# Scores directly behind the probabilities, and maxima ahead of the other VectorE work, in the first cross attention of a two-layer decoder

## The chip, the cores and the metric

The kernel is one program on one core of a Trainium2 chip. Its time is the device time of one execution in microseconds (us), and a time given for a kernel is the median of several executions. A profiled execution is one more execution of the same program, taken by the hardware profiler. The engines are called as in the profile: PE is TensorE (PEld its weight loads), DVE is VectorE, ACT is ScalarE, POOL is GpSimd and SP is SyncE, which issues most DMAs. Each engine takes its instructions in the order in which they were written, and engines wait for one another on semaphores.

## What is computed

Sixteen sequences of 100 tokens of width 256 go through two decoder layers. Each layer is a mixer, a cross attention over 361 context rows and a mixture of experts, each added to its input. The change lies in the first layer's cross attention, which runs once for each of the 16 sequences:

```python
x = x + _L0_attn_ref(_layernorm(x, axis=-1), ...)          # gated recurrence and MLP
x = x + _L0_xattn_ref(_layernorm(x, axis=-1), ctx_1024, ctx_1024, ...)   # <- the change is in here
x = x + _L0_ffn_ref(_layernorm(x, axis=-1), ...)           # 32 experts, top 4, capacity, and a shared expert
x = x + _L1_attn_ref(...); x = x + _L1_xattn_ref(...); x = x + _L1_ffn_ref(...)

def _L0_xattn_ref(query, key, value, Wq, bq, Wk, bk, Wv, bv, Wo, bo):      # 16 heads of 16
    q, k, v = split(query @ Wq.T + bq), split(key @ Wk.T + bk), split(value @ Wv.T + bv)
    weights = softmax(einsum('bhqd,bhkd->bhqk', q, k) * inv_sqrt_d)
    out = einsum('bhqk,bhkd->bhqd', weights, v)
    return join(out) @ Wo.T + bo
```

## The kernel before

`stage_cross_experts` holds the first cross attention and, behind it, the first mixture of experts. The attention runs over 16 sequences `b`, and each sequence over 12 slots `k` (4 quarters of 4 heads, times 3 pieces of the 361 keys). In slot `k` PE makes one unit of scores in key-major form, ACT takes their exponential, and these are the probabilities of that slot (`prob_unit`, L2617; ACT L2866). The softmax needs the maximum of each row first. So one sequence ahead PE makes the scores of sequence `b + 1` in token-major form, in eight units `u` of two heads (`score_unit`, L2584), and VectorE takes their maxima (DVE L3031). After the last unit VectorE splits the maxima into two bfloat16 parts (`split_shift`, L3039 and L3041), PE turns them over (`shift_rows`, L2603), and ACT copies them in as extra rows of the queries (L2890), so that the next sequence's probabilities come out with the maximum taken off.

The eight score units go through four banks of `ps_score`, two banks to a unit: unit `u` waits until VectorE has the maximum of unit `u - 2` (semaphore `v_max`). Units 0 and 1 wait instead for ACT's copies of this sequence's values and shift rows out of the same banks (`a_val`, `a_shift`; ACT L2876 and L2890).

Beside this each slot has other work, set by the tables at the head of the stage. PE: `weigh_values` (L2630, slots 1, 4, 7 and 10), `logits` of sequence `b - 2` (L2671, slot 2, waits for ACT's copy L2885), for some sequences `positions`, `to_rows` of sequence `b - 1` (L2643, slot 4), `turn` (L2649, slot 6), `project` (L2657, slot 8), `values` of sequence `b + 1` (L2597, slots 9 to 11) and `turn_normal` of sequence `b - 1` (L2664, slot 11). VectorE: `to_rows` (L3047, L3049, slot 4), `project` of sequence `b - 1` (L3055 and statistics L3058, slot 8), `moments` (L3062, L3064, slot 9), `normalise` (L3073, slot 10), and in nine of the sequences parts of the routing, one part behind the other work of every second slot or so.

POOL has three things that hang on these. `set_base(b + 1)` (L3341) waits until VectorE has finished `project` of sequence `b - 1` (`v_out`). From sequence 8 on two indirect DMAs that scatter routing rows stand next in POOL's queue (`scatter`, L3366), and only then `root(b - 1)` (L3348), for which VectorE's `normalise` waits, and PE's `turn_normal` waits for that.

The tables and the order of the calls within a slot on PE, before:

```python
SCORE_AT = {0: 0, 2: 1, 3: 2, 4: 3, 5: 4, 6: 5, 7: 6, 8: 7}
AV_AT = {4: 0, 7: 1, 10: 2}
LAST_AV, SHIFT_B, SCALED, ROWS, TURN, OUT, SHIFT = 1, 0, 3, 4, 6, 8, 11
```

Below, "unit 3" is `score_unit(b + 1, 3)`, and the nine sequences 5 to 7, 9 to 11 and 13 to 15 are those with routing parts on VectorE.

## Time and profile before

| | us |
|---|---|
| median of 3 runs | 1654.94 |
| lowest, highest | 1651.81, 1658.08 |
| profiled execution, its own time | 1658.24 |
| its span, first to last instruction | 1656.1 |
| PE busy | 1481.8 (89%) |
| VectorE busy | 788.9 (48%) |
| ACT busy | 704.6 (43%) |
| POOL busy | 480.0 (29%) |

The span is what the instructions of the profiled execution took; 2.1 us lie around it. PE's clock was granted at 0.960 of full speed on the mean. The first cross attention is the stretch from 276.58 to 536.28 us, 259.7 us for the 16 sequences; sequence `b` is counted here from PE's first probabilities of that sequence to those of the next one.

### The profile page before, as it was taken

What the parts mean: (1) busy time and instruction counts of PE and PEld (TensorE: products, weight loads), DVE (VectorE), ACT (ScalarE), POOL (GpSimd) and SP (SyncE); (2) the same over time, 40 slices, a digit from 0 to 9 for tenths busy, and PEclk for the clock granted to TensorE, in tenths of its full rate; (3) what the DMA queues carried; (4) which work ended last, traced back from release to release, by engine and by line L of the source; (5) the groups of instructions that cost most, each with busy time, mean ns of one, the idle gap of its engine ahead of it and who ended that gap; (6) DMA issues with size and microseconds to landing.
All of it is one profiled execution on the core that took longest, in us unless ns stands there. A gap on an engine that the chain in (4) does not pass through costs nothing. (4 is left out here: it accounts for less than half of the span.)

```text
span 1656.1 us, 30297 instructions
## 1 busy us (share of the span) xinstructions
PE 1481.8 (89%) x11672; PEld 1113.7 (67%) x11672; DVE 788.9 (48%) x2238; ACT 704.6 (43%) x1473; POOL 480.0 (29%) x428
## 2 busy tenths in 40 slices
PE   6999997998887999999999957898799999949986
PEld 3666665666565668888888834565467667639885
DVE  6577575567665422222212236765566766541111
ACT  3463465666655212222222234455655565612222
POOL 2122122111434545666666520111101111012232
PEclk9999998999999999999999977999899999969999
DMA  7342567798671217777777626458477776439995
GB/s 300 124 147 94 161 159 127 139 158 139 111 127 34 78 47 192 195 197 192 192 199 201 151 52 160 80 107 166 93 144 128 121 129 121 74 102 345 312 301 159
DMA packets 252439, 250.86 MB, mean 151 GB/s; under 512 B 116724, under 2 KB 226700, under 8 KB 246796
## 3 DMA queue, kind: packets, MB, share of 16 engines
q1 hardware_dynamic: 210316, 221.13, 52.7%
q0 software_dynamic: 41984, 27.84, 9.8%
q8 instruction: 93, 1.52, 0.4%
q14 instruction: 46, 0.38, 0.1%
HBM read 194.10 MB, written 54.58 MB: 150 GB/s over the span
## 5 line engine op out<-in xcount | busy, mean ns | idle before, releaser
L2836 PE MATMUL cross_ps_score<-cross_q,cross_k 128*128 128x250 f32 x1024 | 221.8, 374 | 0.8 <-DVE cross_q L3317 0.8
L2836 PEld LDWEIGHTS cross_ps_score<-cross_q,cross_k 128*128 128x128 f32 x1024 | 194.3, 190 | 23.5 <-DVE cross_q L3317 1.0
L3326 DVE TENSOR_TENSOR cross_prob<-cross_act_,cross_ps_score 128x250 f32<-128x250 f32 x128 | 53.2, 416 | 266.7 <-ACT cross_act_ L3004 265.4
L1746 ACT ACTIVATE layer_parts<-layer_ps_prob 128x400 f32<-128x400 f32 (+1 forms) x192 | 97.0, 508 | 104.7 <-PE layer_ps_prob L1562 102.7
L3031 DVE TENSOR_REDUCE cross_nmax<-cross_ps_score 100x2 f32<-100x722 f32 x128 | 111.7, 902 | 61.0 <-PE cross_ps_score L2584 57.9
L3417 POOL DMA_INDIRECT x_sum<-cross_ye,cross_token x64 | 128.6, 2010 | 37.4 <-issue 19.0
L2866 ACT ACTIVATE cross_prob<-cross_ps_prob 128x400 f32<-128x400 f32 (+1 forms) x192 | 96.2, 508 | 93.4 <-PE cross_ps_prob L2617 91.8
L3004 ACT ACTIVATE cross_act_<-cross_ps_score 128x250 f32<-128x250 f32 x128 | 48.6, 380 | 179.0 <-PE cross_ps_score L2836 163.3
L2848 PE MATMUL cross_ps_prob<-cross_val,cross_prob 128*125 128x256 f32 x512 | 115.8, 379 | 0.0
L3407 POOL DMA_INDIRECT cross_xe<-ln_rows,cross_token x64 | 79.8, 1247 | 121.9 <-PE cross_ps_misc L2822 97.2
L3595 ACT ACTIVATE experts_h<-experts_ps_h,experts_b 128x128 f32<-128x128 f32 x160 | 45.7, 368 | 134.8 <-PE experts_ps_h L3564 122.7
L2848 PEld LDWEIGHTS cross_ps_prob<-cross_val,cross_prob 128*125 128x125 f32 x512 | 93.5, 188 | 12.8
L929 PE MATMUL mixer_bank<-mixer_ctx,packed_sb 128*128 128x361 f32 x256 | 86.7, 482 | 2.5 <-ACT xt L833 2.2
L1968 DVE CUSTOM_DVE_ANT_0 packed_sb<-layer_ps_score,layer_mask 100x361 bf16<-100x361 f32 x128 | 63.0, 532 | 38.3 <-PE layer_ps_score L1519 37.9
L3366 POOL DMA_INDIRECT row_token<-cross_choice,cross_row_put x64 | 64.5, 1008 | 31.6 <-issue 14.0
L1968 DVE CUSTOM_DVE_ANT_0 packed_sb<-layer_ring,layer_mask 100x361 bf16<-100x361 f32 x128 | 62.7, 528 | 22.0 <-PE layer_ring L1519 22.0
L3010 ACT ACTIVATE cross_ye<-cross_ps_prob,cross_weight 125x256 f32<-125x256 f32 x64 | 30.4, 474 | 94.4 <-PE cross_ps_prob L2848 92.6
L929 PEld LDWEIGHTS mixer_bank<-mixer_ctx,packed_sb 128*128 128x128 f32 x256 | 49.0, 196 | 30.4 <-issue 5.4
L814 ACT ACTIVATE mixer_full<-mixer_bank,packed_sb 128x361 f32<-128x361 f32 x64 | 34.8, 561 | 78.4 <-PE mixer_bank L929 78.4
L1557 PE MATMUL layer_ps_prob<-consts_sb,layer_mask 100*128 100x400 bf16 x192 | 64.1, 334 | 3.9 <-ACT layer_parts L1746 1.1
L1562 PEld LDWEIGHTS layer_ps_prob<-layer_m_q,layer_stacks 128*128 128x128 bf16 x720 | 51.9, 98 | 23.1
L3530 POOL DMA_INDIRECT out<-experts_ye,experts_put x20 | 31.7, 1587 | 111.2 <-DMA out<-experts_ye,experts_put 103.7
(471 smaller groups left out, 3097.1 us busy)
## 6 DMA issues: line engine op xcount, KB each, us to landing
packed_sb<-in_w SPq DMA_DIRECT2D x20, 1024.0 KB
experts_w<-in_w SPq DMA_DIRECT2D x20, 1024.0 KB
k_stack<-mixer_part SPq DMA_DIRECT2D x32, 541.5 KB, 4.0
cross_k<-in_wg SPq DMA_DIRECT2D x32, 512.0 KB
cross_k<-in_wu SPq DMA_DIRECT2D x32, 512.0 KB
cross_val<-in_wd SPq DMA_DIRECT2D x32, 512.0 KB
layer_stacks<-k_stack SPq DMA_DIRECT2D x30, 270.8 KB, 5.2
cross_k<-k_stack SPq DMA_DIRECT2D x25, 270.8 KB
```

The source lines that it names most:

```text
L929: ins = nc.tensor.matmul(bank[6 + m][:, 0:S2], prog.w(f"{LAYERS[l][1]}_wk", KD)[:, k, m * P:(m + 1) * P], ctx[s][:, k, :], start=(k == 0), ...
L1557: nc.tensor.matmul(ps_prob[k % 2][:, 0:GT], mask[b % M_BUFFERS][:, at:at + P], prog.c("tile_diag")[0:T, :], start=True, stop=False)
L1746: nc.scalar.activation(m_prob_sb[0:rows_, q4 % 2, t, :], ps_prob[k % 2][0:rows_, 0:GT], ACT.Exp, scale=DH ** -0.5).then_inc(m_prob, 1)
L1968: ins = nc.vector.tensor_tensor_reduce(m_scratch[:, h % HH, :], m_score[(u % 2) * 2 + j][0:T, 0:S2], mask[b % M_BUFFERS][:, 0:S2], -1.0, - ...
L2836: ins = nc.tensor.matmul(ps_pre[m][:, side, 0:CAP], w[s][:, k, m * P:(m + 1) * P], xt[s][:, k, :], start=(k == 0), stop=(k == KD - 1))
L2848: ins = nc.tensor.matmul(ps_sum[s][t][0:HALF], up[s][:, m, t * HALF:(t + 1) * HALF], wd[s][:, m, :], start=(m == 0), stop=(m == NUP - 1))
L2866: nc.scalar.activation(prob[0:rows_, q4 % 2, t, :], ps_prob[k % 2][0:rows_, 0:GT], ACT.Exp, scale=DH ** -0.5).then_inc(a_prob, 1)
L3031: nc.vector.tensor_reduce(nmax[b % 2][:, 2 * u:2 * u + 2], ps_score[0:T, (u % 2) * 2:(u % 2) * 2 + 2, 0:S2], AX.X, ALU.max, negate=True).t ...
L3326: nc.vector.tensor_tensor(up[s][:, m, :], act_[:, m % 2, :], ps_pre[m][:, 1, 0:CAP], ALU.mult).then_inc(v_gated[m][s], 1)
L3366: g.indirect_dma_start(prog.row_token, bass.IndirectOffsetOnAxis(row_put[:, c:c + 1], 0), choice[:, c, :], None).then_inc(scattered, 16)
L3407: g.indirect_dma_start(xe[s][:, t, :], None, prog.ln_rows, bass.IndirectOffsetOnAxis(token[:, 2 * e + t:2 * e + t + 1], 0)).then_inc(rows_ ...
L3417: g.indirect_dma_start(prog.x_sum, bass.IndirectOffsetOnAxis(token[:, 2 * e + t:2 * e + t + 1], 0), ye[s][:, t, :], None, compute_op=ALU.a ...
```

## The change

Two calls move within their slot. On PE, `score_unit(b + 1, ...)` is now called directly behind `prob_unit(b, k)`, ahead of the weighted values, logits, positions, rows, turn and project of that slot (and, in sequence 0, ahead of the turn and the projection of the spare queries). On VectorE, `score_unit(b + 1, ...)`, with `split_shift` behind the last unit, is now called ahead of `to_rows` and `project`. No instruction is added or removed, no table changes, and every wait stays with its instruction.

```diff
@@ PE
                         prob_unit(b, k)
                         if b == 0 and k == 0:
                             pe.wait_ge(consts_set, 1)
+                        if b + 1 < B and k in SCORE_AT:
+                            score_unit(b + 1, SCORE_AT[k])
                         if b == 0 and k in Q_TURN_AT:
                             query_turn(Q_TURN_AT.index(k))
...
                         if k == OUT and b > 0:
                             project(b - 1)
                         if b + 1 < B:
-                            if k in SCORE_AT:
-                                score_unit(b + 1, SCORE_AT[k])
                             if k == SHIFT:
@@ VectorE
+                        if b + 1 < B and k in SCORE_AT:
+                            score_unit(b + 1, SCORE_AT[k])
                         if k == ROWS and b > 0:
                             to_rows(b - 1)
                         if k == OUT and b > 0:
                             project(b - 1)
-                        if b + 1 < B and k in SCORE_AT:
-                            score_unit(b + 1, SCORE_AT[k])
```

PE, sequence 12, slots 2 to 4, before. L2617 are the probabilities, L2671 the logits, L2584 a unit of scores, L2630 the weighted values, L2643 the rows:

```order
L2617 MATMUL cross_ps_prob<-cross_q,cross_k 128x100 x4
L2671 MATMUL cross_ps_misc<-cent_t,xt 100x40 x2
L2584 MATMUL cross_ps_score<-cross_k,cross_q 128x361 x2
L2617 MATMUL cross_ps_prob<-cross_q,cross_k 128x100 x4
L2584 MATMUL cross_ps_score<-cross_k,cross_q 128x361 x2
L2617 MATMUL cross_ps_prob<-cross_q,cross_k 128x100 x4
L2630 MATMUL cross_ps_acc<-cross_prob,cross_val 32x100 x12
L2643 MATMUL cross_ps_misc<-packed_sb,cross_acc 100x128 x4
L2584 MATMUL cross_ps_score<-cross_k,cross_q 128x361 x2
```

The same stretch now:

```order
L2617 MATMUL cross_ps_prob<-cross_q,cross_k 128x100 x4
L2584 MATMUL cross_ps_score<-cross_k,cross_q 128x361 x2
L2671 MATMUL cross_ps_misc<-cent_t,xt 100x40 x2
L2617 MATMUL cross_ps_prob<-cross_q,cross_k 128x100 x4
L2584 MATMUL cross_ps_score<-cross_k,cross_q 128x361 x2
L2617 MATMUL cross_ps_prob<-cross_q,cross_k 128x100 x4
L2584 MATMUL cross_ps_score<-cross_k,cross_q 128x361 x2
L2630 MATMUL cross_ps_acc<-cross_prob,cross_val 32x100 x12
L2643 MATMUL cross_ps_misc<-packed_sb,cross_acc 100x128 x4
```

Unit 1 stands ahead of the logits, and unit 3 ahead of the weighted values and the rows; unit 2 has no other work in its slot and stays.

VectorE, sequence 12, slots 2 to 9, before. L3031 are maxima, L3047 and L3049 `to_rows`, L3055 and L3058 `project`, L3039 and L3041 the split, L3062 and L3064 `moments`:

```order
L3031 TENSOR_REDUCE cross_nmax<-cross_ps_score 100x2 x3
L3047 RECIPROCAL cross_rden<-cross_ps_misc 100x16
L3049 TENSOR_TENSOR cross_rows<-cross_ps_misc,cross_rden 100x256
L3031 TENSOR_REDUCE cross_nmax<-cross_ps_score 100x2 x4
L3055 TENSOR_TENSOR packed_sb<-cross_ps_misc,cross_base 100x256
L3058 BN_STATS cross_stats<-packed_sb 100x6
L3031 TENSOR_REDUCE cross_nmax<-cross_ps_score 100x2
L3039 CAST cross_split<-cross_nmax 100x16
L3041 TENSOR_TENSOR cross_split<-cross_nmax,cross_split 100x16
L3062 BN_AGGR cross_mv<-cross_stats 100x2
L3064 TENSOR_SCALAR cross_var<-cross_mv 100x1
```

The same stretch now:

```order
L3031 TENSOR_REDUCE cross_nmax<-cross_ps_score 100x2 x4
L3047 RECIPROCAL cross_rden<-cross_ps_misc 100x16
L3049 TENSOR_TENSOR cross_rows<-cross_ps_misc,cross_rden 100x256
L3031 TENSOR_REDUCE cross_nmax<-cross_ps_score 100x2 x4
L3039 CAST cross_split<-cross_nmax 100x16
L3041 TENSOR_TENSOR cross_split<-cross_nmax,cross_split 100x16
L3055 TENSOR_TENSOR packed_sb<-cross_ps_misc,cross_base 100x256
L3058 BN_STATS cross_stats<-packed_sb 100x6
L3062 BN_AGGR cross_mv<-cross_stats 100x2
L3064 TENSOR_SCALAR cross_var<-cross_mv 100x1
```

The maximum of unit 3 stands ahead of `to_rows`, and the maximum of unit 7 and both instructions of the split stand ahead of `project`.

## Rows read from the trace of the kernel before

**Rows 1.** Span and granted clock of the core.

```profile
core 0: 1656.1 us, clock 0.960
```

**Rows 2.** Stretches by sequence (3, 7, 9 to 12): length, then busy us (count) by engine.

```profile
326.35:341.15 14.80, 13.62 (x189) 9.98 (x189) 9.34 (x17) 9.58 (x24) 2.07 (x4) 1.00 1.08 213
...
386.86:403.35 16.49, 14.37 (x204) 10.72 (x203) 11.47 (x29) 9.68 (x24) 2.07 (x4) 1.00 0.70 125
...
419.28:435.64 16.36, 13.98 (x189) 9.96 (x189) 11.45 (x36) 9.62 (x24) 6.16 (x8) 1.00 0.77 125
435.64:452.41 16.77, 14.04 (x190) 10.03 (x191) 12.16 (x35) 10.55 (x26) 6.16 (x8) 1.00 0.80 120
452.41:470.47 18.06, 14.42 (x205) 10.60 (x204) 11.39 (x30) 9.30 (x23) 6.16 (x8) 1.00 0.66 113
470.47:486.38 15.91, 13.85 (x189) 9.92 (x190) 9.35 (x17) 9.62 (x24) 6.16 (x8) 1.00 0.76 128
```

**Rows 3.** Waits, 296 to 520 us: engine and line, releaser, us, times, longest.

```profile
DVE cross_nmax L3031 <- PE cross_ps_score L2584: 50.1, 31, 6.0
DVE cross_xf L3073 <- POOL cross_rstd L3348: 18.4, 14, 2.4
```

**Rows 4.** PE by time, sequence 12: start, us, instruction, count [idle before, releaser].

```profile
473.13 0.55 PE L2671 MATMUL cross_ps_misc<-cent_t,xt 128*100 128x40 f32 x4 [0.58 <-ACT xt L2885]
473.51 0.48 PE L2584 MATMUL cross_ps_score<-cross_k,cross_q 96*128 96x361 bf16 x2
...
476.74 0.37 PE L2649 MATMUL cross_ps_misc<-packed_sb,cross_rows 100*128 100x100 f32 x2
477.54 0.48 PE L2584 MATMUL cross_ps_score<-cross_k,cross_q 96*128 96x361 bf16 x2 [0.43 <-DVE cross_nmax L3031]
...
481.91 0.72 PE L2630 MATMUL cross_ps_acc<-cross_prob,cross_val 128*32 128x100 f32 x24
```

**Rows 5.** VectorE by time, sequence 12.

```profile
474.03 1.73 DVE L3031 TENSOR_REDUCE cross_nmax<-cross_ps_score 100x2 f32<-100x722 f32 x2 [1.65 <-PE cross_ps_score L2584]
...
480.48 0.42 DVE L3055 TENSOR_TENSOR packed_sb<-cross_ps_misc,cross_base 100x256 f32<-100x256 f32 x1 [0.25 <-PE cross_ps_misc L2657]
...
481.28 0.89 DVE L3031 TENSOR_REDUCE cross_nmax<-cross_ps_score 100x2 f32<-100x722 f32 x1
482.21 0.17 DVE L3039 CAST cross_split<-cross_nmax 100x16 bf16<-100x16 f32 x1
...
482.51 0.17 DVE L3062 BATCH_NORM_AGGREGATE cross_mv<-cross_stats 100x2 f32<-100x6 f32 x1
```

**Rows 6.** ACT by time, then POOL, sequence 12.

```profile
472.48 0.37 ACT L2876 COPY cross_val<-cross_ps_score 105x256 f32<-105x256 f32 x1
...
484.98 0.50 ACT L2866 ACTIVATE cross_prob<-cross_ps_prob 105x400 f32<-105x400 f32 x1 [2.19 <-PE cross_ps_prob L2617]
...
482.02 1.00 POOL L3366 DMA_INDIRECT row_token<-cross_choice,cross_row_put  x1 [0.31 <-POOL cross_base L3341]
483.33 0.99 POOL L3366 DMA_INDIRECT row_token<-cross_choice,cross_row_put  x1 [0.30 <-issue]
```

**Rows 7.** Sequence 10 by time: PE, VectorE, POOL and ACT.

```profile
447.72 0.72 PE L2630 MATMUL cross_ps_acc<-cross_prob,cross_val 128*32 128x100 f32 x24
...
452.18 0.39 PE L2664 MATMUL cross_ps_misc<-packed_sb,cross_xf 100*128 100x100 f32 x2 [1.29 <-DVE cross_xf L3073]
...
447.23 0.42 DVE L3055 TENSOR_TENSOR packed_sb<-cross_ps_misc,cross_base 100x256 f32<-100x256 f32 x1
...
448.77 1.00 POOL L3366 DMA_INDIRECT row_token<-cross_choice,cross_row_put  x1 [0.31 <-POOL cross_base L3341]
...
449.73 0.50 ACT L2866 ACTIVATE cross_prob<-cross_ps_prob 105x400 f32<-105x400 f32 x1 [1.13 <-issue]
```

**Rows 8.** PE by time: the spare queries' turn in sequence 0; unit 0 in sequence 4.

```profile
284.51 0.93 PE L2719 MATMUL cross_ps_misc<-packed_sb 100*128 100x100 f32 x4 [1.89 <-DVE packed_sb L3215]
...
342.81 0.48 PE L2584 MATMUL cross_ps_score<-cross_k,cross_q 96*128 96x361 bf16 x2 [1.30 <-DMA cross_k<-k_stack]
```

## The prediction

> **What bounds the kernel now.** I read the span first: 1656.1 us of the profiled execution, whose own time is 1658.24, 3.3 above the median of 1654.94 [rows 1]. My sum is made on the span, and its difference goes onto the median. Only the first cross attention is touched. Cut into its sequences, the attention shows two regimes [rows 2]. A sequence without routing ahead of number 8, such as 3, takes 14.80 us, of which PE is busy 13.62: PE sets the pace there, and what is left to win is 1.2 us. From sequence 8 on the same work takes 15.91 (number 12), with routing 16.36 to 18.06, while PE's busy time hardly moves (13.85 to 14.42). Something else ends last there.
>
> The waits name it [rows 3]. VectorE waits 50.1 us for scores, which looks like the prize, but it is idle time of an engine busy for 9.3 to 12.2 of some 16 us per sequence. The 18.4 us that `normalise` waits for POOL's root are another matter. In sequence 10 VectorE's `project` starts at 447.23, POOL's first scatter at 448.77, and PE's `turn_normal` runs at 452.18 after 1.29 idle [rows 7]: from `project` to `turn_normal` 4.95, and to the next sequence at 452.41 [rows 2] 5.18. In sequence 12 `project` starts at 480.48 [rows 5] and the next sequence at 486.38 [rows 2]: 5.90. I looked at all seven sequences, 8 to 14: two (10, 14) have 5.2, five have 5.8 to 5.9. So in these seven **the next sequence starts a fixed time after VectorE's `project`**, since base, two scatters, root, `normalise` and `turn_normal` hang on it in a row.
>
> Why two values: in sequence 12 ACT's exponential of the last slot starts at 484.98 after 2.19 idle, although PE made those probabilities at about 483.6; it comes 0.66 after the second scatter ended [rows 6]. In sequence 10 it comes at 449.73, in the middle of the first scatter, not late [rows 7]. The difference I find is when PE starts the third weighted values: 0.11 ahead of the first scatter in sequence 12 (481.91 and 482.02, [rows 4, 6]), 1.05 ahead in sequence 10 (447.72 and 448.77, [rows 7]). What PE signals in between seems to arrive late if those values run into the scatter. I can't say why, but can use it: **late kind** (5.9) and **clear kind** (5.2).
>
> **The change part by part.** Nothing is added, so only order counts. I replay one sequence, from PE's first probabilities at 0.
>
> *Unit 1 ahead of the logits.* PE idles 0.58 ahead of the logits of sequence 12, which start at 473.13, 2.66 after the start; unit 1 starts at 3.04 and VectorE's maximum at 3.56 [rows 4, 5]. Unit 1 itself needs the bank that ACT empties at 472.85, 2.38 after the start [rows 6]. So it starts at 2.43, its maximum at about 2.80: **VectorE is 0.75 ahead**. PE gains less: the unit occupies 0.32 (473.51 to the next row's start), the logits then start at 2.75 instead of 2.66, and the probabilities of slot 4 wait for the exponential of slot 2, which ACT, busy without a gap here, ends no earlier than 3.7. I keep 0.08 for PE.
>
> *Unit 5 ahead of the turn.* Before, PE idles 0.43 ahead of unit 5, waiting for the maximum of unit 3 [rows 4]. Now unit 3's maximum is taken ahead of `to_rows` and 0.75 earlier: that wait goes. But the turn needs `to_rows`, which is now behind the maximum: my replay has the rows ready at 6.4 and the turn at 6.5 instead of 6.27 (476.74), and the probabilities of slot 7 at 6.89 instead of 7.39.
>
> *Units 6 and 7 directly behind the probabilities.* Here the change takes cover away. Unit 6 waits for the maximum of unit 4, and the weighted values (0.66) and the project (0.9) no longer run meanwhile. One maximum takes 0.82 in a row of them (1.73 for two, overlapping). In sequence 3 or 12 this costs 0.15 at unit 6; with a routing part between the maxima, up to 0.35 at unit 7. Queued behind unit 7 on PE stand the project and all values of the next sequence. Net for PE: 0.35 earlier in a sequence without routing, 0.1 to 0.3 with it.
>
> *`project` behind the maximum of unit 7 and the split.* From the start of that maximum to the end of the split VectorE needs 1.23 (481.28 to 482.51, [rows 5]). `project` and its waiters, POOL's base, the scatters and the root, fall behind that. Against it stands the lead of 0.75, and where VectorE had waited for PE's project (0.25 in sequence 12) that gap too. Sum by kind:
> - sequences 8 and 12 (no routing): `project` at 9.95 instead of 10.01, so 0.06 less. The values now start 0.4 ahead of the scatter, still nearer to the late kind; next start 0.06 to 0.08 less.
> - 9 and 13: `project` 0.55 later (1.23 less the lead of about 0.7). The values are then 1.3 ahead of the scatter: the clear kind, 0.65 back. Each 0.10 less.
> - 10 and 14: 0.49 later, clear already, nothing to give back: each **0.48 more**.
> - 11: either unit 1's maximum leads here too (its `project` 0.2 later, clear: 0.5 less) or its signal is held by the scatters of slots 1 to 3 (0.5 more). I take 0.
> Together 8 to 14: -0.14 - 0.20 + 0.96 + 0 = **+0.6**.
>
> *Sequences 0 to 7.* Here the scatters don't exist, and `normalise` has about 0.9 of slack in sequence 3, so the later `project` is hidden by the values of slots 9 to 11; without that cover it would cost the same 0.5. Sequence 2 gains 0.35. So would 3, but 4 waits 1.30 for keys from DMA [rows 8], whose transfers start with sequence 3, so 3 gives its gain back; 4 gains 0.3. 5 and 6 gain 0.2 and 0.25. 7, whose unit 1 stood behind logits and positions, 0.4. 1 gains 0: two wide subtractions on VectorE stand between its maxima. In 0, unit 5 goes into the 1.89 that PE idles ahead of the spare queries' turn [rows 8], and a later wait for ACT's copy takes half of it back: 0.3. Sequence 15 makes no scores. Together **-1.8**.
>
> The waits that SP's queue holds (the stores of `normalise`'s rows, the next keys) move by these same tenths.
>
> *A rule weighed.* In sequence 12 the first scatter, with the split's cast inside it, took 1.00, and the second, with none, 0.99 [rows 5, 6]. The Trainium skill (SBUF — State Buffer, section "Who interferes with whom") says that casts on VectorE can take the port pair that it shares with GpSimd, and whoever starts first then blocks the other for the whole instruction. The change moves the split out of the scatters. By that rule up to a cast of 0.17 would come back in each of seven sequences, 1.2 us in all; by the rows 0.01 each. The sum goes by the rows.
>
> **Sum.** +0.6 - 1.8 = -1.2 on the span: 1654.9, and 1654.94 - 1.2 = 1653.7 for the median. Bounds of what the trace doesn't show: sequences 8 and 12 turning clear would give 0.7 each; 9 and 13 staying late would cost 0.65 each; 11 is 0.5 either way; PE's tenths in 0 to 7 lie between 0 and 0.7 a sequence. That is 1649.5 to 1657. The runs before spread by 3 to either side of their median.
>
> **The rivals.**
> *It works in full.* PE's waits for maxima vanish and nothing comes in their place: 0.35 in each of 14 sequences, 4.9, and the five late sequences turn clear, 3.5: 1646.5. For it: all scatters do move away from the values if `project` moves later. Against it: `project` moves later, and PE's start then doesn't count. From the point where `project` doesn't move and the scatter is still clear, it decides. Chance 0.12.
> *POOL's chain pays in full (slower).* Place: `project` behind unit 7's maximum and the split, sequences 8 to 14. If VectorE's lead doesn't come, because unit 1's signal reaches it no earlier than before (ACT's copies, or the scatters of slots 1 to 3), `project` is 1.23 later in each of seven: +8.6, with nothing won in 0 to 7, 1663.5; with half of the lead gone and the late kind cleared, some 1659. For it: VectorE is busy without a gap from unit 1's maximum to `project` in the routing sequences, so nothing there gives way. Against it: in sequence 12 VectorE did see unit 1's scores as soon as they were made (474.03), between scatters. It decides once less than about 0.5 of the 0.75 arrives. Chance 0.13.
> *The order doesn't matter.* The waits just change places and all ends within a few tenths, 1654.9. This lies inside my forecast's range.
> *Clock.* Granted clock falls to half at 284.5 in sequence 0, behind the 1.89 idle. A unit of scores in that gap may or may not shift this; it is worth up to 1 us either way. Chance that it decides: 0.03.
>
> **How the numbers follow.** Forecast 1653.7 with chance 0.72 (the unmoved case within it), the full gain 0.12, POOL's chain 0.13, the clock 0.03. A range of 1648 to 1659.5 holds the forecast with its bounds and the runs' spread, and leaves out most of the full gain and about two thirds of the slow case: some 0.2. A measurement of this kernel can tell about 0.5% from no change, 8.3 us. Below 1646.7 lies about half of the full gain, 0.06; above 1663.2 a little under half of the slow case, 0.05; the rest, 0.89, is no change that can be told.
>
> **What would show it.** Right: unit 1 on VectorE 2.8 after the start of a sequence; unit 5's wait for maxima gone and a wait of the turn for rows (L2649 behind L3049) in its place; units 6 and 7 waiting for maxima in routing sequences; `project` 0.5 later in 10 and 14 and these sequences 0.5 longer; 9 and 13 of the clear kind; sequences 2 to 7 shorter by 0.2 to 0.4. Wrong: sequences 8 to 14 shorter by more than PE's tenths (then the chain from `project` isn't what starts the next sequence), or sequence 3 longer (then the lost cover of units 6 and 7 weighs more than the removed wait), or a difference outside the first attention.

## The result and the profile after

| | median | lowest to highest | runs |
|---|---|---|---|
| before | 1653.91 us | 1646.31 to 1664.28 | 22 |
| the change | 1658.96 us | 1652.13 to 1664.62 | 22 |

The ratio is 1.0037, with a 95% interval of 1.0024 to 1.0051. The change is slower, by 5 to 6 us, where the prediction had it 1.2 us faster. The time lies in the forecast's range, just under its upper end; the sign was wrong.

First the span and the clock of the change (before: [rows 1]), then its stretches by sequence (before: [rows 2]), from sequence 0 to 14. The columns are start and end, length, busy us (count) of PE, PEld, VectorE, ACT and POOL, granted clock, DMA share, GB/s.

```profile
core 0: 1656.8 us, clock 0.950
```

```profile
278.83:297.40 18.57, 16.10 (x166) 10.23 (x165) 11.51 (x27) 11.25 (x22) 1.74 (x2) 0.91 0.90 150
...
326.94:341.50 14.56, 13.68 (x189) 9.69 (x189) 9.36 (x17) 9.53 (x24) 2.07 (x4) 1.00 1.08 212
...
386.38:404.73 18.35, 16.13 (x203) 11.28 (x204) 11.68 (x29) 9.68 (x24) 2.07 (x4) 0.91 0.62 115
...
420.56:436.74 16.18, 13.74 (x191) 9.63 (x190) 11.37 (x36) 9.79 (x24) 6.15 (x8) 1.00 0.75 125
436.74:453.88 17.14, 13.96 (x192) 9.65 (x191) 12.52 (x36) 9.90 (x25) 6.13 (x8) 1.00 0.81 119
453.88:473.69 19.81, 17.40 (x206) 12.28 (x204) 11.67 (x30) 9.90 (x24) 6.14 (x8) 0.83 0.60 102
473.69:489.00 15.31, 13.58 (x191) 9.60 (x190) 9.37 (x18) 9.79 (x24) 6.14 (x8) 1.00 0.81 133
```

Two stretches stand out. Sequence 7 takes 18.35 (16.49 before) and 11 takes 19.81 (18.06), and both have a granted clock under 1.00, which none of the sequences 1 to 14 had before. Sequence 3 is 0.24 shorter, 9 and 12 are 0.19 and 0.60 shorter, 10 and 14 are 0.37 and 0.51 longer. (By the same profiles 4 is 0.63 shorter, 0 is 1.43 shorter, and 14, at 0.99, has a fallen clock in its last tenths.)

What happened in sequence 7 around unit 6, by time, and then VectorE ahead of it (start, us, instruction, idle before and releaser):

```profile
395.91 0.91 DVE L3031 TENSOR_REDUCE cross_nmax<-cross_ps_score 100x2 f32<-100x722 f32 x1
396.05 0.13 PEld L2584 LDWEIGHTS cross_ps_score<-packed_sb,up 96*128 96x128 bf16 x2 [1.36 <-DVE cross_nmax L3031]
396.06 0.79 PE L2584 MATMUL cross_ps_score<-packed_sb,up 96*128 96x361 bf16 x2 [1.22 <-DVE cross_nmax L3031]
...
396.77 1.23 PE L2630 MATMUL cross_ps_acc<-cross_prob,cross_val 128*32 128x100 f32 x24
```

```profile
393.50 0.25 DVE L3047 RECIPROCAL cross_rden<-cross_ps_misc 100x16 f32<-100x16 f32 x1
393.78 0.42 DVE L3049 TENSOR_TENSOR cross_rows<-cross_ps_misc,cross_rden 100x256 f32<-100x256 f32 x1
394.12 0.36 DVE L3155 TENSOR_REDUCE cross_prior_add<-cross_any_hot 100x32 f32<-100x128 bf16 x1
394.40 0.68 DVE L3157 TENSOR_REDUCE cross_pos<-cross_prod 100x16 f32<-100x512 f32 x1
394.99 0.19 DVE L3159 TENSOR_TENSOR cross_prior<-cross_prior,cross_prior_add 100x32 bf16<-100x32 bf16 x1
395.09 1.72 DVE L3031 TENSOR_REDUCE cross_nmax<-cross_ps_score 100x2 f32<-100x722 f32 x2
```

Unit 6 now stands directly behind the probabilities and waits 1.22 for the maxima of unit 4. VectorE takes them at 395.09, behind the rows and part 11 of the routing (394.12 to 395.09). Behind the wait PE's matmuls are slow: the pair of scores takes 0.79 where it takes 0.48 elsewhere, the weighted values 1.23 where they took 0.72 [rows 4]. A mean clock of 0.91 over 18.35 us is some 3.4 us at the lower level, 1.2 GHz.

Sequence 11 has two such stretches. The second lies behind unit 6's wait, as in 7. The first begins with the sequence, behind another wait: `turn_normal`, the last work of sequence 10, waits 2.06 for `normalise`, where it waited 1.29 [rows 7].

```profile
453.65 0.40 PE L2664 MATMUL cross_ps_misc<-packed_sb,cross_xf 100*128 100x100 f32 x2 [2.06 <-DVE cross_xf L3073]
```

```profile
453.88:457.31 3.43, 3.43 (x42) 2.53 (x41) 0.91 (x2) 3.10 (x9) 2.08 (x4) 0.50 0.68 137
...
464.14:467.55 3.41, 3.31 (x34) 2.13 (x35) 2.28 (x8) 0.50 (x1) 0.00 (x0) 0.50 0.93 121
```

By this one pair of profiles the attention (sequences 0 to 14) takes 242.9 us before and 243.7 after, 0.7 more. The medians are 5 apart. So there were two questions: do sequences 7 and 11 decide, and where do the other 4 us come from?

### The profile page after: what moved, and what is told of

It reads as the page before. It is cut to its first block and busy times, and to the rows that moved or that the text cites. A ratio compares the mean times of both kernels' runs of the same rounds, so it can differ in the third digit from the quotient of the medians.

```text
span 1656.8 us, 30297 instructions
## 1 busy us (share of the span) xinstructions
PE 1492.4 (90%) x11672; PEld 1118.3 (67%) x11672; DVE 790.9 (48%) x2238; ACT 703.5 (42%) x1473; POOL 478.8 (29%) x428
## 5 line engine op out<-in xcount | busy, mean ns | idle before, releaser
L3031 DVE TENSOR_REDUCE cross_nmax<-cross_ps_score 100x2 f32<-100x722 f32 x128 | 111.8, 903 | 50.8 <-PE cross_ps_score L2584 50.5
```

What stands on the lines that cost most here:

```text
L3031: nc.vector.tensor_reduce(nmax[b % 2][:, 2 * u:2 * u + 2], ps_score[0:T, (u % 2) * 2:(u % 2) * 2 + 2, 0:S2], AX.X, ALU.max, negate=True).t ...
```

## The experiments

These theories were put up. **A**: sequences 7 and 11 (the wait for unit 4's maxima and the clock). **B**: POOL's chain in 8 to 14, fed later because `project` stands behind unit 7. **C** and **L**: outside the attention. **M**: ordinary executions of the attention are worse than the profiled one. All times of sequences are from one profile of each kernel. Steps (a) to (d) in the expectations are the four paragraphs of the prediction's change part by part: unit 1, unit 5, units 6 and 7, `project`. A condition in a diff stands on both engines unless it says otherwise, and the old place has the opposite condition.

### One engine, or one kind of sequence

`positions_old` keeps the old order in the sequences with `positions` (7, 11 and 15), `positions_new` has the new order in them alone:

```diff
-if b + 1 < B and k in SCORE_AT:
+if b + 1 < B and k in SCORE_AT and counted_group(b) is None:      # positions_old
+if b + 1 < B and k in SCORE_AT and counted_group(b) is not None:  # positions_new
     score_unit(b + 1, SCORE_AT[k])
```

`tensor_half` has the diff's two hunks in PE's loop, `vector_half` its two hunks in VectorE's.

> The change as it is, but with before's order on TensorE and VectorE in the three sequences of the first attention that also make the positions (7, 11 and 15). Theory A (the whole loss sits in sequences 7 and 11: TensorE waits 1.2 us for the maxima of unit 4 behind the rows and a part of the routing on VectorE, and its granted clock falls to half): no slower than before, 1651 to 1654 us (before 1653.9, the change 1659.0), lengths of sequences 7 and 11 back at 16.5 and 18.1 us (18.4 and 19.8 with the change). Theory B (`project` behind the maxima of unit 7 on VectorE feeds GpSimd later in sequences 8 to 14): still 3 to 5 us slower than before. Theory C (clock or transfers outside these sequences): still 3 to 5 us slower, and the mean granted clock stays at 0.953 instead of 0.96.

> The counterpart: the change in sequences 7, 11 and 15 alone, all others in before's order. Theory A: the whole loss or more, 1657 to 1660 us, sequences 7 and 11 1.7 to 1.9 us longer each than in before, with TensorE's granted clock at half for 3 to 10 us in them. Theory B and theory C: within 1 us of before (1653 to 1655).

> TensorE's half of the change alone: the next sequence's scores directly behind the probabilities, with VectorE in before's order. Theory A: TensorE waits even longer for the maxima of unit 4 (behind the rows, and of unit 3, now behind the rows as before), so slower than the change: 1660 to 1664 us. Theory B: VectorE's `project` is ahead of the maxima of unit 7 again, so this is the better half: 1652 to 1655 us.

> VectorE's half alone: the maxima ahead of the rows and of `project`, TensorE in before's order. Theory A: without scores directly behind the probabilities TensorE has its weighted values and `project` as cover for the maxima, so no clock drop in sequences 7 and 11 and 1652 to 1655 us. Theory B: `project` is behind the maxima of unit 7 and its scores come last on TensorE, so GpSimd's chain gets it later still: 1657 to 1662 us.

| kernel | ratio to before | 95% interval | attention, us | sequence 7 | 11 |
|---|---|---|---|---|---|
| positions_old | 0.9986 | 0.9960 to 1.0011 | 240.4 | 16.50 | 17.95 |
| positions_new | 1.0021 | 1.0004 to 1.0039 | 246.7 | 18.52 | 18.51 |
| tensor_half | 1.0039 | 1.0014 to 1.0064 | 254.1 | 16.91 | 21.54 |
| vector_half | 1.0089 | 1.0057 to 1.0122 | 255.4 | 16.75 | 20.35 |

With the old order in three sequences the loss is gone, and with the new order in those three alone there is one. That speaks for theory A, but not as cleanly as it looks. In `positions_new` sequence 7 is 2.0 longer, as theory A wants, and 11 only 0.4: unit 6 waits 1.21 there too, but the clock stays whole. Another 1.8 of its 3.8 us lie in sequence 10, which has the old order; there the clock fell with no idle time of PE over 0.75 just ahead of it:

```profile
438.24 0.39 PE L2664 MATMUL cross_ps_misc<-packed_sb,cross_xf 100*128 100x100 f32 x2 [0.75 <-ACT cross_prob L2868]
439.10 0.35 PE L2617 MATMUL cross_ps_prob<-cross_q,cross_k 128*128 128x100 bf16 x4 [0.47 <-ACT cross_q L2892]
```

```profile
439.10:457.62 18.52, 15.58 (x189) 11.03 (x190) 12.16 (x35) 10.59 (x26) 6.17 (x8) 0.91 0.66 109
```

Nor is theory B refuted: these four ran on a chip where sequences in the old order are of the late kind (8 and 9 of `positions_new`: 5.87 and 5.80 from `project` to the next start), so the new order of `positions_old` had something to win back there that it hasn't everywhere, as the last group of runs shows. Both halves alone have a longer attention than the whole (243.7); as kernels only `vector_half` is clearly the slower one, `tensor_half` comes out at 1.0039 like the change. For both I had named one theory under which they would be the better half: B for `tensor_half`, A for `vector_half`, and both missed. `tensor_half` waits 0.95 for maxima that VectorE still takes late; `vector_half`'s turn waits 1.08 for rows:

```profile
448.38 0.48 PE L2584 MATMUL cross_ps_score<-packed_sb,up 96*128 96x361 bf16 x2 [0.95 <-DVE cross_nmax L3031]
```

```profile
449.28 0.39 PE L2649 MATMUL cross_ps_misc<-packed_sb,cross_rows 100*128 100x100 f32 x2 [1.08 <-DVE cross_rows L3049]
```

### The change taken back step by step, on one chip

`part_later` is the change with part 11 of the routing one slot later. `part_later_7_old` also puts unit 7 back behind `project` from sequence 5 on. `slots_to_6` is the change for units 1 to 5 alone. `change_again` is the change itself.

```diff
-    ROUTE_AT = (0, 2, 4, 6, 8, 10, 12, 14, 16, 20, 23, 25, 27, 28, 30, 32)
+    ROUTE_AT = (0, 2, 4, 6, 8, 10, 12, 14, 16, 20, 23, 26, 27, 28, 30, 32)   # part_later, part_later_7_old
...
-if b + 1 < B and k in SCORE_AT:
+if b + 1 < B and k in SCORE_AT and (b <= G or k < 8):   # part_later_7_old
+if b + 1 < B and k in SCORE_AT and k < 7:               # slots_to_6
```

> The change once more, beside the three below. Theory A (sequences 7 and 11): again 0.2 to 0.5% slower than before, sequence 7 about 18.4 us and sequence 11 18.5 to 19.8 us long, the other thirteen together 2 to 3 us shorter than in before. If it comes out level with before, the loss hangs on the execution and not on the order.

> The change, with part 11 of the routing one slot later on VectorE (slot 5 instead of 4, in sequences 7, 11 and 15 alone), so that the maxima of unit 4 come 1.0 us earlier. Theory A, by VectorE's queue: TensorE's wait for them in sequences 7 and 11 falls from 1.22 us to 0.2 to 0.4, the granted clock stays whole, the sequences are back at 16.3 to 16.6 and 17.9 to 18.1 us, and the kernel is 3 to 5 us faster than the change, 0.1 to 0.2% under before. Rival A2 (the bare order on TensorE does it, with no weighted values ahead of unit 6): the sequences stay over 17.5 and 19 us.

> The change on both engines for slots 2 to 6 alone (units 1 to 5); units 6 and 7 stay behind the weighted values and `project`, as in before, in all sequences. Theory A and A2 alike: sequences 7 and 11 at 16.3 to 16.5 and 17.8 to 18.1 us. Steps (b) and (c) of the prediction: the light sequences keep 0.1 to 0.3 us each, since their gain comes with unit 5. Step (d): sequences 10 and 14 back at 16.8 us, since `project` is ahead of the maxima of unit 7. The kernel 2 to 3 us under before (0.998 to 0.999).

> The change with part 11 one slot later and, from sequence 5 on, with unit 7 behind `project` on both engines as in before. If theory A and step (d) both hold, the best of the lot: sequences 7 and 11 at 16.3 and 17.9 us, 10 and 14 at 16.8, the rest as in the change; all of the attention 2.8 to 3.5 us shorter than in before, so 1.5 to 4 us off the kernel. If sequences 10 and 14 stay at 17.1 and 17.3 us, step (d) has the wrong cause.

| kernel | median | ratio to before (1652.36) | 95% interval | attention |
|---|---|---|---|---|
| change_again | 1657.93 | 1.0044 | 1.0024 to 1.0063 | 243.7 |
| part_later | 1655.22 | 1.0028 | 1.0010 to 1.0046 | 239.4 |
| part_later_7_old | 1648.00 | 0.9974 | 0.9960 to 0.9988 | 231.3 |
| slots_to_6 | 1645.30 | 0.9955 | 0.9936 to 0.9974 | 230.4 |

Part 11 alone gives 2.7 us back (4.3 by the profiles), unit 7 behind `project` 7.2 (8.1), the last step 2.7 (0.9). That last step is not unit 6 alone: it also takes unit 7 back in sequences 0 to 4 and part 11 to its old slot. `part_later` missed its expectation, 0.1 to 0.2% under before: it is 0.28% over it, with the wait of unit 6 gone. Of its 4.3, 2.2 lie in sequence 11, and not all of these are part 11's. Here `turn_normal` of sequence 10 waits the same 2.06, and this time no fall of the clock follows; part 11 stands further down in sequence 11, so it is no direct cause of that. **The largest loss is in neither sequence 7 nor 11 but in all of 8 to 14, and unit 7 causes it**: my expectation for `slots_to_6` had been 2 to 3 us under before, and it is 7. Lengths by sequence show where; `before_third` is a profile of the kernel before that comes up below.

| sequence | before | before_third | change | part_later | part_later_7_old | slots_to_6 |
|---|---|---|---|---|---|---|
| 0 | 20.00 | 21.53 | 18.57 | 18.57 | 18.55 | 18.86 |
| 2 | 14.84 | 14.84 | 14.61 | 14.62 | 14.62 | 14.24 |
| 4 | 15.24 | 14.84 | 14.61 | 14.61 | 14.69 | 14.74 |
| 6 | 15.49 | 15.49 | 15.34 | 15.34 | 15.01 | 14.88 |
| 7 | 16.50 | 16.50 | 18.36 | 16.48 | 16.18 | 16.19 |
| 8 | 15.93 | 15.44 | 15.83 | 15.83 | 15.26 | 14.83 |
| 9 | 16.37 | 15.45 | 16.18 | 16.18 | 14.95 | 14.94 |
| 10 | 16.76 | 16.51 | 17.13 | 17.12 | 15.91 | 15.91 |
| 11 | 18.07 | 16.71 | 19.81 | 17.64 | 16.41 | 16.40 |
| 12 | 15.91 | 14.92 | 15.31 | 15.31 | 14.75 | 14.32 |
| 8 to 14 | 116.2 | 111.0 | 117.7 | 115.4 | 108.1 | 107.9 |

In `part_later` unit 6 of sequence 7 waits 0.24 instead of 1.22, and the values behind it take their 0.72:

```profile
393.85 0.48 PE L2584 MATMUL cross_ps_score<-packed_sb,up 96*128 96x361 bf16 x2 [0.24 <-DVE cross_nmax L3031]
394.27 0.72 PE L2630 MATMUL cross_ps_acc<-cross_prob,cross_val 128*32 128x100 f32 x24
```

So it is VectorE's queue ahead of the maxima, and not the bare order on PE, that opened the wait (theory A over A2).

What unit 7 costs is seen in sequence 9 (`part_later_7_old` has the same 14.95 there with unit 6 in its new place), VectorE by time, first the change, then `slots_to_6` (its lines are 2 further down):

```profile
430.33 0.90 DVE L3031 TENSOR_REDUCE cross_nmax<-cross_ps_score 100x2 f32<-100x722 f32 x1
431.57 0.42 DVE L3055 TENSOR_TENSOR packed_sb<-cross_ps_misc,cross_base 100x256 f32<-100x256 f32 x1
...
436.05 0.41 DVE L3073 TENSOR_SCALAR cross_xf<-packed_sb,cross_mv,cross_rstd 100x256 f32<-100x256 f32 x1 [2.69 <-POOL cross_rstd L3348]
```

```profile
426.19 0.42 DVE L3057 TENSOR_TENSOR packed_sb<-cross_ps_misc,cross_base 100x256 f32<-100x256 f32 x1
...
430.66 0.41 DVE L3075 TENSOR_SCALAR cross_xf<-packed_sb,cross_mv,cross_rstd 100x256 f32<-100x256 f32 x1 [1.59 <-POOL cross_rstd L3352]
```

`project` starts 11.01 after the sequence's start (431.57 - 420.56) with the change and 9.77 (426.19 - 416.42) without unit 7 ahead of it; from there `normalise` follows at 4.48 and 4.47, and the next sequence at 5.17 in both. 1.24 later `project`, 1.24 longer sequence: POOL's chain, theory B.

### Short kernels and single units

The short kernels leave out the second layer and the last experts and copy the first experts' sum to the output:

```diff
-    stage_layer1(prog)
-    stage_experts1(prog)
+    with stage(nc, "copy") as (sem, sbuf, psum):
+        copied = sem("copied")
...
+                sp.dma_start(out, prog.x[3]).then_inc(copied, 16)
```

`unit_1_early` has the new order for `k < 3`, `unit_7_early` for `k == 8` alone.

> The kernel before without its second layer and last experts (some 680 us of its 1656): it ends with the first experts and copies their sum to the output, so its output is not the reference's. About 980 us. It is the base for the next one: theory L says that what the change loses beyond the first attention comes behind the first experts, theory M says that executions without a profile lose it in the first attention.

> The change, cut short in the same way. The traces of the whole kernels say +0.7 us in the first attention, -1.3 in its last sequence and +1.2 in the first experts. Theory L: 0.3 to 1.5 us above the short kernel before, since the rest of the 5.1 us comes later. Theory M: 4 to 6 us above it.

> The change in slots 0 and 2 alone: unit 1's scores ahead of `logits` on TensorE, its maxima where they were in effect on VectorE. Step (a): the sequences without routing as in before, those with it 0 to 0.1 us shorter, the kernel within 1 us of before (0.9994 to 1.0006). Sequence 0 stays at 20.0 us. Rival: unit 1 is what opens the wait ahead of the maxima in the sequences with routing, and 8 to 14 each come out 0.5 to 0.9 us shorter, 4 to 6 us in all.

> Slot 8 of the change alone: unit 7's scores directly behind the probabilities, ahead of `project`, and VectorE takes their maxima ahead of `project`; everything else as in before. Step (d): sequences 1 to 6 as in before, 8 to 14 each 0.5 to 1.3 us longer (late `project`, late chain on GpSimd), 5 to 8 us in all, the kernel at 1.003 to 1.005 of before. Rival (what costs is unit 6 behind the rows, not unit 7): within 1 us of before in all of them.

The medians of the short kernels are 981.11 us (5 runs, 978.74 to 985.58) and 982.55 (6 runs, 975.83 to 987.04): 1.4 more, which theory L expected (0.3 to 1.5) and theory M did not. But the runs of the short change spread over 11 us. Its profile holds a useful chance: in sequence 7 unit 6 waits the same 1.22, and this time the clock stays up.

```profile
386.57:403.49 16.92, 14.70 (x204) 10.44 (x204) 11.59 (x29) 9.70 (x24) 2.07 (x4) 1.00 0.68 125
```

```profile
396.25 0.48 PE L2584 MATMUL cross_ps_score<-packed_sb,up 96*128 96x361 bf16 x2 [1.22 <-DVE cross_nmax L3031]
```

16.48 without the wait (`part_later`), 16.92 with it, 18.36 with it and a fallen clock: **the wait costs 0.44, the clock behind it 1.44**, and the second comes in some executions only: with this order in sequence 7 the clock fell in 4 profiles of 5. In sequence 11 it fell in all four profiles of the change, each time near the start, behind the 2.06 to 2.07 of `turn_normal`, and in two of them once more behind unit 6; in `change_third` it stayed down for 10.2 us and unit 6 waited only 0.32, and the sequence still took 19.79. Where sequence 10 has unit 7 behind `project` on both engines, `turn_normal` waits 1.17 to 1.31, and no fall followed in any of the ten profiles. By these counts a good part of the loss in sequence 11 is unit 7's, through the clock.

`unit_1_early`: 0.9992 (0.9972 to 1.0013). Sequences 2, 3, 5, 8, 9 and 12 stay within 0.1 of before: unit 1 alone brings them nothing, as expected; 6, 7 and 14 win 0.3 to 0.4, more than I had given it, and 10 loses 1.5 with a fallen clock. `unit_7_early`: 1.0025 (0.9998 to 1.0052), attention 248.8, sequences 8 to 10 at 16.34, 16.70 and 17.75, and 11 at 20.29 with 10.2 us of lower clock. All seven, 8 to 14, are together 5.2 us longer than in before: at the lower end of what B expected. The kernel itself isn't told from before with certainty. This profile's fall in sequence 11, too, begins 0.36 into it, behind 2.07 of `turn_normal`.

### The other 4 us

> The kernel before, once more, as a kernel of its own. By theory L (stages behind the first experts add an amount that each execution draws anew) within 0.15% of before, and its trace shows the attention at 242 to 243 us with the part behind the last projections (186 to 191 us in the traces so far) at another value.

> The change on the same chip as the kernel before. If the extra 4 us belong to the change: 1.003 to 1.005 of before. If they belong to the executions drawn so far: 1.000 to 1.002, what the traces show (+0.7 us in the attention, +0.6 with its last sequence and the first experts).

> Slots 2 to 6 of the change alone, without the second layer and the last experts, as the two short kernels (981.1 and 982.6 us) were. The trace of the whole kernel has its attention at 230.4 us and its last sequence at 15.0 (before 242.9 and 16.8), the first experts 1.2 us longer. Theory L: 967 to 970 us, the whole gain arrives. Theory M (ordinary executions of the attention are worse than the profiled ones): 973 us or more.

> The change with part 11 one slot later, and from sequence 5 on VectorE alone takes `project` ahead of the maxima of unit 7, while TensorE still makes unit 7's scores ahead of `project`. If VectorE's order is what sequences 8 to 14 pay for: 9 and 13 at 15.0 to 15.3 us, as with both engines in the old order (14.95; 16.2 with both in the new). If TensorE's order pays (0.6 us of scores ahead of `project`): 15.5 to 15.8 us, half of it. The kernel 1648 to 1653 us where before is 1652.

`project_first` differs from `part_later` on VectorE alone:

```diff
-if b + 1 < B and k in SCORE_AT:
+if b + 1 < B and k in SCORE_AT and (b <= G or k < 8):   # VectorE only
```

`before_again`, the kernel before compared with itself, comes out at 0.9992 (0.9975 to 1.0010), with the attention at 242.1 us. `change_third` is at 1.0019 (0.9994 to 1.0045) with 246.8: here sequence 4 takes 17.46 instead of 14.61, since PE waits for the next keys and the clock falls behind that wait:

```profile
344.99 0.48 PE L2584 MATMUL cross_ps_score<-cross_k,cross_q 96*128 96x361 bf16 x2 [2.24 <-DMA cross_k<-k_stack]
```

```profile
342.40:359.86 17.46, 14.91 (x189) 10.91 (x190) 9.44 (x17) 10.05 (x24) 2.07 (x4) 0.90 0.81 142
```

`slots_6_short` has a median of 976.25 (6 runs), 4.9 under the short kernel before, where theory L wanted 11 to 14. Its attention took 237.0, not 230.4: sequence 4 again (16.91), and sequences 8, 9 and 11 to 13 are of the prediction's late kind, 5.74 to 5.92 from `project` to the next start, although the very same order had 5.17 in `slots_to_6`. `project_first` (0.9999, 0.9979 to 1.0018) shows it too: `project` of sequence 9 at 10.39, half-way between 9.77 and 11.01; but the next start follows 5.76 behind, and the sequence takes 16.15 as in the change, outside both expectations. That each engine's order pays 0.62 doesn't follow, since `project` of 9 also comes 0.26 later behind a sequence of the late kind (10.28 in `before_third`, 10.54 in before). Sequences 5 and 6, ahead of all scatters, compare cleanly (`part_later_7_old`, `project_first`, `part_later`): TensorE's order pays 0.36 and 0 there (10.03 to 10.39, 10.98 to 10.98), VectorE's 0.87 and 1.24 (to 11.26 and 12.22). The two kinds for one order asked for the last two, the same kernels once more on one chip:

> Slots 2 to 6 of the change alone, once more. If the 5.2 us from `project` to the next start in sequences 8, 9 and 11 to 13 belongs to this order, it shows again and the attention takes 230 to 232 us. If it goes with the chip or the execution, it may come out at 5.8, as in the short kernel, with 234 to 237 us. The kernel 0.993 to 0.997 of before either way.

> The kernel before beside it, on the same chip. If the kind belongs to the order: 5.8 to 5.9 us behind `project` in sequences 8, 9 and 11 to 13, attention 242 to 243 us. If it goes with the chip: the same kind as in the run above, and with 5.2 an attention of 239 to 240 us. Its time within 0.2% of before.

`slots_to_6_again` is at 0.9965 (0.9942 to 0.9988), attention 232.6 with a wait of 2.62 for the keys in sequence 4, all of 9 to 14 with 5.2. **`before_third` (1.0009, 0.9985 to 1.0034) has 5.2 as well, with the order of before**: the attention takes 238.9, although sequence 0 took 21.5. Its stretches 9, 11 and 12 (before: [rows 2]):

```profile
422.12:437.57 15.45, 13.65 (x192) 9.95 (x190) 11.20 (x36) 9.84 (x24) 6.15 (x8) 1.00 0.80 131
...
454.07:470.78 16.71, 14.27 (x205) 10.63 (x204) 11.48 (x30) 9.78 (x24) 6.14 (x8) 1.00 0.73 120
470.78:485.70 14.92, 13.52 (x191) 9.89 (x190) 9.36 (x18) 9.61 (x24) 6.14 (x8) 1.00 0.95 137
```

And its sequence 12, PE, POOL and ACT (before: [rows 4, 6]):

```profile
481.96 0.72 PE L2630 MATMUL cross_ps_acc<-cross_prob,cross_val 128*32 128x100 f32 x24
...
482.07 1.00 POOL L3366 DMA_INDIRECT row_token<-cross_choice,cross_row_put  x1 [0.31 <-POOL cross_base L3341]
...
483.97 0.50 ACT L2866 ACTIVATE cross_prob<-cross_ps_prob 105x400 f32<-105x400 f32 x1 [1.13 <-PE cross_ps_prob L2617]
```

The weighted values start 0.11 ahead of the scatter, just as in [rows 4, 6], and ACT's exponential is not late: 13.19 after the sequence's start, against 14.51 there. So the late kind is not a property of the order. I then read the lead of the values over the first scatter, sequences 8 to 14, in all 20 profiles. With a lead of 0.7 or more (in the change, all sequences but 11) the kind was clear in each of them, on every chip: 5.16 to 5.33, and 5.45 in sequence 8. With 0.1 to 0.6 it was late in all of 9 profiles, 8 of them on the chips of the first group and of `before_again`, and clear in all of 6, among them the 5 on the chips of `slots_to_6` and `before_third`. Both kinds came with the same order. Whether the chip itself decides or a state that it happened to be in, these runs don't tell. The ninth late one is the profile of before that the prediction used, and the sixth clear one is the change's own (0.51 in sequence 11, 5.16): the first pair of profiles compared a late execution with a clear one, which hid some 5 us of the loss.

This closes the account as far as it closes. On a chip where before is clear, sequences 8 to 14 take 111.0 in before and 117.7 in the change: +6.7, of which sequence 11 is 3.1. Sequences 2 to 6 give 0.9 back, sequence 7 costs 1.9, and sequence 0, which drew 19.5 to 21.5 in before and 18.5 to 18.6 in the change, gives 1 to 3. That is +4.7 to +6.7, and the medians say 5 to 6. Where before is late, its own sequences 8 to 14 are 5.2 longer, and there `change_third` found the ratio at 1.0019, against 1.0044 on a chip with the clear kind; their intervals overlap, so this difference fits but isn't proven. The medians of before fit as well: 1652.4 and 1655.0 on the two chips whose profiles are clear, 1660.6, 1661.4 and 1663.4 on the two that are late. The 1653.91 of the result lies with the first. Chips may differ in more than this, so that is a sign and no proof. The part from the last projections to the end took between 183 and 195 us in the profiles, and differed as much for one kernel (191, 195 and 186 in three profiles of before). That is why one profile's total can't carry a difference of 5 us, while its sequences can.

## Why the prediction was wrong

*Unit 1 ahead of the logits: right.* Predicted for VectorE: 2.8 after the start. Found in sequence 12 of the change at 476.39, 2.70 after it:

```profile
476.39 2.54 DVE L3031 TENSOR_REDUCE cross_nmax<-cross_ps_score 100x2 f32<-100x722 f32 x3 [1.09 <-PE cross_ps_score L2584]
```

*Unit 5 ahead of the turn: right, but undersized, and what was to follow it didn't.* The wait of 0.43 [rows 4] is gone. `slots_to_6` shows units 1 to 5 worth 0.5 to 0.6 in most sequences, with routing (15.45 to 14.94 in sequence 9) and without it (14.84 to 14.24 in 2), where I had 0.35 and 0.1 to 0.3; it is 0.3 in 7 and 11, and nothing in 1. The turn's wait for rows, which I had put in its place, did not appear. Sequence 0, booked at 0.3, gave 1.4 (20.00 to 18.57).

*Units 6 and 7 directly behind the probabilities: the step that failed first.* I priced the lost cover at 0.15 without routing and up to 0.35 with it. Unit 6 alone costs 0.43 in 8 and 12 and nothing in 9 and 10 (`part_later_7_old` less `slots_to_6`); in 2, where that pair differs in unit 7 too, both cost 0.38. In 7 and 11, which I booked at -0.4 and 0, the change takes 1.9 and 2.2 more than `part_later`; in 7 that is the wait and the clock behind it, in 11 a fall of the clock behind `turn_normal` is in it too. My replay took one sequence with a short routing part and carried it over; it never put part 11 (0.97) and the rows together ahead of unit 4's maxima in the two sequences that have both. The clock rival was priced at 1 us and tied to sequence 0, where PE had idled; I didn't ask whether the change makes a new idle stretch of that length elsewhere. It makes two: unit 6's 1.22, and `turn_normal`'s, which grows from 1.29 to 2.06 in sequences 10 and 14.

*`project` behind unit 7: right in its size, wrong in its balance.* I had `project` 0.55 later in 9 and 0.49 in 10. It came 0.47 and 0.38 later (10.54 to 11.01, 11.59 to 11.97), against a before of the late kind; against `before_third` it is 0.73 and 0.64. But the balance was "lead less price", and the lead was won by units 1 to 5 without unit 7. Priced by itself, unit 7 costs 1.21 to 1.25 in each of 9, 10, 11, 13 and 14, and 0.57 in 8 and 12.

*Late kind and clear kind: the step that turned the sign.* I credited 9 and 13 with 0.65 each for turning clear, and they did: 5.17. Against the profile of before that made my -0.10 look right (-0.19 and -0.16 measured). But I took the kind for a property of the order, from one execution. Where before is clear, there is nothing to get back: sequence 9 is 0.7 longer with the change, and 8 to 14 together 6.7, where I had +0.6. Even with unit 6's wait removed (`part_later`) the kernel is slower there, 1.0028. On a late chip the sign isn't settled: the interval of `change_third` includes 1.

*The rivals.* "POOL's chain pays in full" had the mechanism and the place, and 8.6 for seven sequences; unit 7's price there is 7.3 (`part_later` less `part_later_7_old`). Its condition was wrong: VectorE's lead did arrive. It decides whenever nothing is to be had from the late kind. "It works in full", 4.9 for PE's waits, is what `slots_to_6` does, without unit 7 and unit 6.

*A rule weighed.* The first scatter of sequence 9 in the change, with no cast in it any more, took 1.00, as one did with a cast in it, in sequence 12 of before [rows 6]. The rule of the Trainium skill on the shared port pair (SBUF — State Buffer, "Who interferes with whom") would have moved the sum by at most 1.2 us and shows no effect here.

```profile
433.11 1.00 POOL L3366 DMA_INDIRECT row_token<-cross_choice,cross_row_put  x1 [0.31 <-POOL cross_base L3341]
```

Still open: what makes the short lead late on one chip and not on another, why the clock falls behind a wait in one execution and not in the next, and how often ordinary executions draw the wait for the keys in sequence 4 (2.2 to 2.9 us longer in `change_third`, `slots_6_short` and `slots_to_6_again`, 0.4 in two profiles of before, nothing in `before_third`).

## What to carry to other kernels

When a move has several steps, price each against the version without it, not against the kernel before: units 1 to 5 won 7 us, units 6 and 7 lost them again, and a net sum near zero hid both. A step that takes cover away from a wait has to be replayed in every kind of iteration, the heaviest first, and a new idle stretch of TensorE, like the 1.22 and 2.06 us here, should carry the price of the lower clock beside its own, as a chance and not as a certainty. And before a gain is booked on a pattern in one profile, look at a second execution of the same kernel.

## What the runs showed of the hardware

- The same wait of 1.22 us on TensorE was followed by 3.4 us at the lower granted clock in one execution and by none in another; the fall cost 1.44 us, over three times the 0.44 us that the wait itself cost.
- The clock's fall isn't tied to one wait: behind `turn_normal`'s 2.06 to 2.07 us at the end of sequence 10 it fell in five profiles of the seven with unit 7 ahead of `project` on both engines, and in `positions_new` and `unit_1_early` it fell in sequence 10 with no idle time over 0.76 us just ahead.
- With the weighted values starting 0.1 to 0.6 us ahead of GpSimd's scatter, ACT's exponential behind them came 1.3 us later in some profiles than in others, for identical instructions (14.51 and 13.19 after the start); in the profiles whose chip is known, two chips were always late and two never. With 0.7 us or more it was never late.
- Where nothing is late, the next sequence starts 5.16 to 5.20 us behind VectorE's `project` in 9 to 13, in every order tried: the chain through GpSimd is the steadiest number of this kernel.
